# First stage: latents and rotary keys from rounded-32-bit parts, and the next chunk's rows transposed between the rotary queries and the queries' content

## The chip, the core and the metric

The program runs on one core of a Trainium2 chip. The metric is the device time of one launch in microseconds, so lower is better. The engines are TensorE (PE for its matmuls, PEld for its weight loads), VectorE (DVE), ScalarE (ACT), GpSimd (POOL) and SyncE (SP), which issues most DMAs. Each works through its own list of instructions in order, and they meet at semaphores.

## What is computed

An embedding lookup, one attention layer with low-rank (latent) queries, keys and values, and one mixture-of-experts layer, for 4 sequences of 2048 tokens of 256 numbers. All is 32-bit. The part that the change touches is the projection ahead of the attention:

```python
h = take(weight, x)                      # (4, 2048, 256)
n = layernorm(h)
ct_q  = n @ Wd_q + b;    ct_kv = n @ Wd_kv + b            # latents, 128 wide
query = heads(ct_q @ Wu_q + b) + heads(rope(ct_q @ Wq_r + b))
key   = heads(ct_kv @ Wu_k + b) + heads(rope(n @ Wk_r + b))
value = heads(ct_kv @ Wu_v + b_v)
out   = softmax(query key^T / scale) value                # 16 heads of 16
h = h + out @ Wo + b_o
h = h + moe(layernorm(h))                # 32 experts, top 1, 320 slots each
```

## The kernel before

Four stages follow each other: the projections (first stage), the attention, the router, the experts. The time up to about 284 us is the first stage, the attention lasts to about 2914 us, the router to about 3060 us.

**The first stage** goes through 16 chunks of 512 tokens (four sequences b, four chunks k in each; this text numbers them 0 to 15). The orders are written out by hand in one function `chunk` for each engine:

- **POOL**: the two sums of the queries' rotary terms (L395, L396), four gathers of table rows for the chunk three ahead (L357), the low part of the queries (L404, x = 0), the root of the layer norm for the chunk two ahead (`root`: L364, L365, L367, L370), the low part of the keys (L404, x = 1).
- **DVE**: four rotary terms of the queries (L557), the values with their bias (L586), the queries' sum (`full`, L566), the statistics of the chunk two ahead (L545), four rotary terms of the keys (L557), the moments (L549), the two sums of the keys' terms (L598, L599), the keys' sum (L566).
- **ACT**: the copy of the transposed rows (L494), the high part of the queries (`split`, L520), the two latents of the next chunk (L499), the high part of the keys (L520), the normalisation of the chunk two ahead (L507).
- **PE**: rotary queries (L442), the queries' content (L454), values (L459), the transposes of the next chunk's normed rows (L420), rotary keys (L445), the next chunk's latents (L428), the keys' content (L454).
- **SP**: stores the rows, the values (L334) and the parts (L341), each when its semaphore says so.

A query or key leaves the stage as a high part (rounded to fp32r by ACT) and a low part (the rest, by POOL). The low part needs the high part, and the high part needs `full`. The POOL sums of a chunk stand behind the keys' low part of the chunk before. Matmuls on plain 32-bit data show in the trace as two MATMUL records each; those on data marked fp32r (the attention's scores) as one.

**The attention** begins on DVE straight behind its last `full`, with maxima over keys and queries of the first four heads (L1027). POOL multiplies each unit's result by the reciprocals (L824). **The router** has its own `root` on POOL (L1228 to L1234), behind it the scatter of rows to expert slots (L1257).

## Time and profile before

| | us |
|---|---|
| median of 3 runs | 3315.01 |
| lowest and highest | 3313.55 and 3324.78 |
| time of the profiled execution | 3315.87 |
| its span | 3314.0 |

| engine | busy us | share of the span |
|---|---|---|
| PE | 3202.7 | 97% |
| DVE | 2908.6 | 88% |
| ACT | 2468.7 | 74% |
| POOL | 565.3 | 17% |

The profile is one execution. 1.9 us lie around its span. The shares are means over four stages with different limits; the attention alone is four fifths of the time.

### The profile page before, as it was taken

Reading aid. Unit: us, or ns where it says so; the run is one execution under the profiler, and the core shown is the slowest. Engines: PE = TensorE matmul, PEld = TensorE weight load, DVE = VectorE, ACT = ScalarE, POOL = GpSimd, SP = SyncE. Lnnn points to the kernel's source line nnn. Section 1 sums busy time; section 2 is a strip of 40 time slices with the busy share of each in tenths; the row PEclk is TensorE's granted clock in tenths of the full one; section 3 lists DMA queues with packets and bytes.
Section 4 is the critical chain, followed back from the end, with each engine's and each line's share of the span. In section 5 each row is a group of like instructions: output and inputs, shape, how many; then the busy total and the mean of one; then the engine's idle time right before and its main releaser. Section 6 shows DMA issues by size and latency. Waiting matters only on the chain.

```text
span 3314.0 us, 67613 instructions
## 1 busy us (share of the span) xinstructions
PE 3202.7 (97%) x27520; PEld 1369.7 (41%) x27520; DVE 2908.6 (88%) x3157; ACT 2468.7 (74%) x4578; POOL 565.3 (17%) x752
## 2 busy tenths in 40 slices
PE   7997999999999999999999999999999999986999
PEld 3443333333333333333333333333333333365666
DVE  6889999999999999999999999999999999567222
ACT  3331888888888888888888888888888888943221
POOL 7882000000000000000000000000000000046233
PEclk9997999999999999999999999999999999998999
DMA  6895213131313131313131313122222220168773
GB/s 201 256 299 159 54 49 72 37 72 37 72 38 72 38 74 38 72 40 72 37 72 39 83 34 79 39 70 44 65 45 58 45 83 21 37 204 305 231 238 101
DMA packets 269155, 305.40 MB, mean 92 GB/s; under 512 B 45270, under 2 KB 198399, under 8 KB 265517
## 3 DMA queue, kind: packets, MB, share of 16 engines
q1 hardware_dynamic: 256812, 271.63, 29.7%
q0 software_dynamic: 12032, 29.45, 2.7%
q8 instruction: 217, 3.56, 0.5%
q14 instruction: 94, 0.76, 0.1%
HBM read 165.81 MB, written 139.23 MB: 92 GB/s over the span
## 4 chain that ended last, share of the span: by engine, by line
PE 81%; ACT 4%; DVE 3%; issue 2%; POOL 1%; DMA 0%; another core or an unknown queue 0%; SPq 0%; POOLq 0%; DVEq 0%
PE ps_o L916 33%; PE ps_s L899 26%; PE ps_m L868 13%; ACT probs L1012 2%; PE ps_g L1592 2%; PE ps_y L1603 2%; PE ps_u L1592 2%; DVE max_parts L1027 2%; ACT weighted L992 1%; PE ps_td L1581 1%; ACT rows_c L1343 1%; POOL slot_rows L1257 0%; PE ps_s L883 0%; POOL shift_c L1234 0%; DVE stats_c L1377 0%
## 5 line engine op out<-in xcount | busy, mean ns | idle before, releaser
L1027 DVE TENSOR_REDUCE max_parts<-ps_m 128x2 f32<-128x1024 f32 x2048 | 2486.1, 1223 | 79.9 <-PE ps_m L868 71.5
L1012 ACT ACTIVATE probs<-ps_s 128x512 f32<-128x512 f32 x4096 | 2217.5, 597 | 312.3 <-PE ps_s L899 127.8
L868 PE MATMUL ps_m<-keys,queries 48*128 48x512 f32 x4096 | 1483.5, 453 | 17.1 <-DVE max_parts L1027 16.7
L899 PE MATMUL ps_s<-queries,keys 51*128 51x512 f32 x4096 | 1480.5, 447 | 9.5 <-ACT probs L1012 3.1
L916 PE MATMUL ps_o<-probs,vals 128*32 128x256 f32 x16384 | 1295.5, 391 | 0.0
L899 PEld LDWEIGHTS ps_s<-queries,keys 51*128 51x128 f32 x4096 | 610.5, 185 | 832.2 <-issue 785.2
L868 PEld LDWEIGHTS ps_m<-keys,queries 48*128 48x128 f32 x4096 | 595.4, 187 | 77.4 <-DVE max_parts L1027 50.2
L916 PEld LDWEIGHTS ps_o<-probs,vals 128*32 128x32 f32 x16384 | 329.4, 108 | 720.4 <-issue 699.0
L824 POOL TENSOR_TENSOR heads_out<-weighted,recip_rows 128x512 f32<-128x512 f32 x63 | 80.9, 1285 | 2147.4 <-DMA recip_rows<-recip_rows_dram 2147.4
L1663 DVE TENSOR_TENSOR hidden<-ps_u,silu 128x320 f32<-128x320 f32 x64 | 31.5, 492 | 127.4 <-PE ps_u L1592 101.6
L1639 ACT ACTIVATE silu<-ps_g 128x320 f32<-128x320 f32 x64 | 28.0, 438 | 134.1 <-PE ps_g L1592 82.8
L520 ACT ACTIVATE parts<-full 128x1024 fp32r<-128x1024 f32 x32 | 33.8, 1057 | 99.7 <-DVE full L566 79.0
L1565 POOL DMA_INDIRECT out<-result,tokens_d x80 | 77.9, 974 | 172.0 <-DVE result L1669 151.9
L1669 DVE SCALAR_TENSOR_TENSOR result<-ps_y,rows_d 128x256 f32<-128x256 f32 x80 | 38.7, 484 | 53.4 <-PE ps_y L1603 49.6
L404 POOL TENSOR_TENSOR parts<-full,parts 128x1024 fp32r<-128x1024 f32 x32 | 75.6, 2363 | 35.7 <-ACT parts L520 35.3
L1343 ACT ACTIVATE rows_c<-resid,shift_c,rstd_c 128x256 f32<-128x256 f32 x64 | 33.2, 589 | 60.5 <-POOL shift_c L1234 60.5
L1592 PE MATMUL ps_g<-rows_td,w_gate 128*128 128x320 f32 x256 | 77.2, 445 | 0.5 <-issue 0.5
L1603 PE MATMUL ps_y<-w_down,hidden 128*64 128x256 f32 x640 | 75.9, 384 | 0.7 <-DVE hidden L1663 0.7
L1592 PE MATMUL ps_u<-rows_td,w_up 128*128 128x320 f32 x256 | 74.1, 432 | 0.0
L566 DVE SCALAR_TENSOR_TENSOR full<-ps_r,b_cols,sums 128x512 f32<-128x512 f32 x64 | 45.1, 747 | 32.0 <-POOL sums L396 29.4
L1271 PE MATMUL ps_p<-w_o,att_t 128*128 128x256 f32 x256 | 64.2, 396 | 7.1 <-DVE resid L1371 6.9
L1633 ACT ACTIVATE rows_td<-ps_td 128x512 f32<-128x512 f32 (+1 forms) x48 | 23.6, 524 | 61.4 <-PE ps_td L1581 61.4
(108 smaller groups left out, 1600.0 us busy)
## 6 DMA issues: line engine op xcount, KB each, us to landing
slot_rows<-empty SPq DMA_DIRECT2D x16, 1290.0 KB, 5.2
vext<-val SPq DMA_DIRECT2D x64, 256.0 KB
halves_q<-parts SPq DMA_DIRECT2D x64, 256.0 KB
halves_k<-parts SPq DMA_DIRECT2D x64, 256.0 KB
keys<-halves_k SPq DMA_DIRECT2D x32, 512.0 KB, 7.5
queries<-halves_q SPq DMA_DIRECT2D x128, 128.0 KB, 3.2
vals<-vext SPq DMA_DIRECT2D x32, 512.0 KB, 5.6
recip_rows<-recip_rows_dram SPq DMA_DIRECT2D x64, 256.0 KB
```

Source lines behind the costliest of these rows:

```text
L404: pool.tensor_tensor(parts[:, k % 2, x, 1].bitcast(F32R), full[:, x], parts[:, k % 2, x, 0], ALU.subtract).then_inc(low_ok[x], 1)
L824: pool.tensor_tensor(heads_out[:, lu % 2, :], weighted[:, lu % 2, :], recip_rows[:, lu % 2, :], ALU.mult).then_inc(heads_ok, 1)
L868: mm = pe.matmul(ps_m[m % 2][:, h, :], queries_r[par][rows, qt, p, t * P:(t + 1) * P], keys_r[par][rows, p, c * 512:(c + 1) * 512], start= ...
L899: pe.matmul(ps_s[bank][:], keys_r[par][rows, p, k * P:(k + 1) * P], queries_r[par][rows, qt, p, :], start=True, stop=True).then_inc(scores ...
L916: mm = pe.matmul(ps_o[32 * j:32 * j + 32, cols], vals[:, par, k, VW * j:VW * (j + 1)], probs[:, (n + j) % RING, cols], start=k == 0 and ha ...
L1012: act.activation(probs[:, n % RING, :], ps_s[bank][:], ACT.Exp, scale=SCALE).then_inc(probs_ok[bank], 1)
L1027: dve.tensor_reduce(max_parts[:, lu % 2, :, p, t, c], ps_m[m % 2][:], AX.X, ALU.max).then_inc(maxima_ok[m % 2], 1)
L1271: mm = pe.matmul(ps_p[:, t // 2, t % 2 * DM:(t % 2 + 1) * DM], att_t[:, k, d, t * P:(t + 1) * P], w_o[:, d, :], start=d == 0, stop=d == KD ...
L1343: act.activation(rows[:, k, t, 0:DM], resid[:, k % 2, t, :], ACT.Identity, bias=shift[:, k % 2, t:t + 1], scale=rstd[:, k % 2, t:t + 1]).t ...
L1565: pool.indirect_dma_start(out, bass.IndirectOffsetOnAxis(ap=tokens[:, k, i:i + 1], axis=0), result[:, k % 2, i, :], None, bounds_check=T - ...
L1592: mm = pe.matmul(bank[m][:, 0:CAP], w[:, k, KD * e + d, m * P:(m + 1) * P], by_half[:, :, e, :], start=d == 0, stop=d == KD - 1)
L1603: mm = pe.matmul(ps_y[n % 2][e * HALF:(e + 1) * HALF, 0:DM], hidden[:, k % 2, e, f, i * HALF:(i + 1) * HALF], w_down[:, k, (FF // P) * e + ...
```

## The change

1. Latents and rotary keys: weights and transposed rows are split into a rounded part and the rest, both fp32r, and each plain matmul becomes three fp32r ones (high by high, low by high, high by low). ACT writes the high rows in its copy, DVE the low rows in a new step `low_rows`. The weights are split once, by DVE at the start.
2. The values lose their bias in the first stage, and ACT copies them (`copy_val`) in place of DVE. POOL adds the bias to each attention result instead (`add_values_bias`, 64 times), from a small table that SP loads at the start of the attention.
3. The layer norm's two small preparations move from POOL to DVE (`root_inputs`), in the first stage and in the router.
4. POOL in the first stage: `root` goes ahead of both low parts.
5. ACT in the first stage: the keys' high part goes behind the next chunk's copy of transposed rows.
6. PE in the first stage: the next chunk's transposes go between the rotary queries and the queries' content, from chunk 1 on.
7. Router on DVE: the moments go ahead of `gate`, and the new `root_inputs` behind it.

```diff
@@ POOL, first stage
 def root(b, k):
-    pool.wait_ge(stats_ok, after(b, k, CT))
-    pool.tensor_tensor(var_eps[:, k, :], mv[:, k, :, 1], eps_sb[:], ALU.add).then_inc(eps_ok, 1)
-    pool.tensor_tensor(neg_mean[:, k, :], no_mean[:], mv[:, k, :, 0], ALU.subtract).then_inc(neg_mean_ok, 1)
     pool.wait_ge(eps_ok, after(b, k))
     pool.tensor_tensor(rstd[:, k, :], var_eps[:, k, :], neg_half[:], ALU.pow).then_inc(rstd_ok, 1)
...
     if ahead:
         gather(*ahead)
+    if not (last and k + 2 >= CPB):
+        root(*((b, k + 2) if k + 2 < CPB else (b + 1, k + 2 - CPB)))
     for x in range(2):
-        if x == 1 and not (last and k + 2 >= CPB):
-            root(*((b, k + 2) if k + 2 < CPB else (b + 1, k + 2 - CPB)))
         pool.wait_ge(high_ok[x], after(b, k))
@@ PE, latent
     for x in range(2):
         for d in range(KD):
-            last = pe.matmul(ps_l[:, x, :], w_down[:, x, d, :], normed_t[:, k % 2, d, :],
-                             start=d == 0, stop=d == KD - 1)
+            for p in range(2):
+                pe.matmul(ps_l[:, x, :], w_down_r[:, p, x, d, :], high_r[:, k % 2, d, :],
+                          start=d == 0 and p == 0, stop=False, skip_group_check=True)
+    pe.wait_ge(nt_low_ok, after(b, k))
+    for x in range(2):
+        for d in range(KD):
+            last = pe.matmul(ps_l[:, x, :], w_down_r[:, 0, x, d, :], low_r[:, k % 2, d, :],
+                             start=False, stop=d == KD - 1, skip_group_check=True)
         last.then_inc(lat_ps, 1)
@@ PE, chunk
     rotary(b, k, 0)
+    early = more and (b, k) != (0, 0)
+    if early:
+        transpose(*nxt)
     content(b, k, 0)
     values(b, k)
-    if more:
+    if more and not early:
         transpose(*nxt)
@@ ACT, chunk
     if more:
         copy_nt(*nxt)
+    if (b, k) != (0, 0):
+        split(*((b, k - 1) if k else (b - 1, CPB - 1)), 1)
+    copy_val(b, k)
     split(b, k, 0)
     if more:
         copy_lat(*nxt)
-    split(b, k, 1)
@@ DVE, first stage
+def root_inputs(b, k):
+    dve.wait_ge(stats_steps, after(b, k, 2 * CT))
+    dve.tensor_scalar(neg_mean[:, k, :], mv[:, k, :, 0], -1.0, None, ALU.mult)
+    dve.tensor_scalar(var_eps[:, k, :], mv[:, k, :, 1], EPS, None, ALU.add).then_inc(eps_ok, 1)
+def low_rows(b, k):
+    dve.wait_ge(nt_ok, after(b, k))
+    dve.tensor_tensor(low_r[:, k % 2], ps_t[:], normed_h[:, k % 2], ALU.subtract).then_inc(nt_low_ok, 1)
...
+dve.wait_ge(w_in, 3 * 16)
+dve.tensor_copy(w_down_r[:, 0], w_down[:]).then_inc(w_split, 1)
+dve.tensor_copy(w_kr_r[:, 0], w_kr[:]).then_inc(w_split, 1)
...
     rope_terms(b, k, 0)
-    dve.wait_ge(val_out[k % 2], uses(b, k, CT * 16))
-    for h in range(2):
-        ...
+    if not (last and k == CPB - 1):
+        low_rows(*((b, k + 1) if k + 1 < CPB else (b + 1, 0)))
     add_content(b, k, 0)
     if ahead:
         row_stats(*ahead)
+        row_moments(*ahead)
+        root_inputs(*ahead)
     rope_terms(b, k, 1)
-    if ahead:
-        row_moments(*ahead)
@@ POOL, attention
+def add_values_bias(pool, step, lu):
+    q = (step * 2 + lu // 4) % (QUADS // BATCH)
+    pool.tensor_scalar(heads_out[:, lu % 2, :], heads_out[:, lu % 2, :], bias_v[:, q:q + 1], None, ALU.add).then_inc(heads_ok, 1)
```

**POOL, one chunk in the middle of the first stage.** `sums` and `parts` are the sums and low parts, `emb` the gathers. Before:

```order
L395 TENSOR_TENSOR sums<-terms 128x512 [waits terms_ok_q,ids_in0,full_ok_q,emb_out0,norm_ok]
L396 TENSOR_TENSOR sums<-terms 128x512
L357 DMA emb<-in_table,ids 128x256 x4
L404 TENSOR_TENSOR parts<-full,parts 128x1024 [waits high_ok_q]
L364 TENSOR_TENSOR var_eps<-mv,eps_sb 128x4 [waits stats_ok]
L365 TENSOR_TENSOR neg_mean<-no_mean,mv 128x4
L367 TENSOR_TENSOR rstd<-var_eps,neg_half 128x4 [waits eps_ok]
L370 TENSOR_TENSOR shift<-neg_mean,rstd 128x4 [waits neg_mean_ok,rstd_ok]
L404 TENSOR_TENSOR parts<-full,parts 128x1024 [waits high_ok_k]
```

After:

```order
L388 TENSOR_TENSOR sums<-terms 128x512 [waits terms_ok_q,ids_in1,full_ok_q,emb_out1,norm_ok]
L389 TENSOR_TENSOR sums<-terms 128x512
L356 DMA emb<-in_table,ids 128x256 x4
L363 TENSOR_TENSOR rstd<-var_eps,neg_half 128x4 [waits eps_ok]
L365 TENSOR_TENSOR shift<-neg_mean,rstd 128x4 [waits rstd_ok]
L396 TENSOR_TENSOR parts<-full,parts 128x1024 [waits high_ok_q]
L396 TENSOR_TENSOR parts<-full,parts 128x1024 [waits high_ok_k]
```

The root now stands between the gathers and the queries' low part, with two operations fewer.

**ACT, one chunk of the first stage.** `parts` with full_ok_q or full_ok_k is the high part of queries or keys. Before:

```order
L494 ACTIVATE normed_t<-ps_t 128x1024 [waits trans_ok]
L520 ACTIVATE parts<-full 128x1024 [waits parts_out0,full_ok_q]
L499 ACTIVATE lat<-ps_l,b_cols 128x512 [waits lat_ps] x2
L520 ACTIVATE parts<-full 128x1024 [waits parts_out0,full_ok_k]
L507 ACTIVATE normed<-emb,shift,rstd 128x256 [waits trans_ok,shift_ok]
```

After:

```order
L500 ACTIVATE normed_h<-ps_t 128x1024 [waits trans_ok]
L534 ACTIVATE parts<-full 128x1024 [waits parts_out0,full_ok_k]
L506 ACTIVATE val<-ps_l 128x32x16 [waits val_ps,val_out1]
L506 ACTIVATE val<-ps_l 128x32x16 [waits val_ps]
L534 ACTIVATE parts<-full 128x1024 [waits parts_out1,full_ok_q]
L512 ACTIVATE lat<-ps_l,b_cols 128x512 [waits lat_ps] x2
L520 ACTIVATE normed<-emb,shift,rstd 128x256 [waits trans_ok,shift_ok]
```

The keys' high part of a chunk now follows the next chunk's copy of transposed rows.

**PE, from the rotary queries of a chunk on.** Before:

```order
L442 MATMUL ps_r<-lat,w_qr 128x512 [waits lat_ok,terms_ok_k]
L442 MATMUL ps_r<-lat,w_qr 128x512
L454 MATMUL ps_r<-lat,w_uq 128x512 [waits full_ok_k]
L454 MATMUL ps_r<-lat,w_uq 128x512
L459 MATMUL ps_l<-w_uv,lat 128x256 x4
L420 MATMUL ps_t<-ident_a,normed 128x128 [waits nt_ok,norm_ok]
L420 MATMUL ps_t<-ident_a,normed 128x128 x7
L445 MATMUL ps_r<-normed_t,w_kr 128x512 [waits terms_ok_q]
```

After:

```order
L443 MATMUL ps_r<-lat,w_qr 128x512 [waits lat_ok,terms_ok_k]
L443 MATMUL ps_r<-lat,w_qr 128x512
L415 MATMUL ps_t<-ident_a,normed 128x128 [waits nt_low_ok,norm_ok]
L415 MATMUL ps_t<-ident_a,normed 128x128 x7
L456 MATMUL ps_r<-lat,w_uq 128x512 [waits full_ok_k]
L456 MATMUL ps_r<-lat,w_uq 128x512
L461 MATMUL ps_l<-w_uv,lat 128x256 x4
L447 MATMUL ps_r<-normed_h,w_kr_parts 128x512 [waits terms_ok_q]
```

The transposes moved ahead of the content and the values.

## Rows read from the trace of the kernel before

**Rows 1.** Chain of waits in time: start us, length us, engine, line, count.

```profile
284.23 36.21 DVE max_parts L1027 x32
```

**Rows 2.** Timeline, POOL, one period: start us, length us, engine, line, operation [idle before].

```profile
229.84 1.26 POOL L396 TENSOR_TENSOR sums<-terms 128x512 f32<-128x512 f32 x1
...
235.11 0.95 POOL L357 DMA_INDIRECT emb<-in_table,ids  x1 [0.31 <-issue]
236.08 2.35 POOL L404 TENSOR_TENSOR parts<-full,parts 128x1024 fp32r<-128x1024 f32 x1
238.41 0.65 POOL L364 TENSOR_TENSOR var_eps<-mv,eps_sb 128x4 f32<-128x4 f32 x1
...
239.61 1.05 POOL L367 TENSOR_TENSOR rstd<-var_eps,neg_half 128x4 f32<-128x4 f32 x1
240.75 0.20 POOL L370 TENSOR_TENSOR shift<-neg_mean,rstd 128x4 f32<-128x4 f32 x1
242.26 2.37 POOL L404 TENSOR_TENSOR parts<-full,parts 128x1024 fp32r<-128x1024 f32 x1 [1.32 <-ACT parts L520]
...
245.82 1.27 POOL L396 TENSOR_TENSOR sums<-terms 128x512 f32<-128x512 f32 x1
```

**Rows 3.** Timeline, DVE, the same period.

```profile
231.19 1.41 DVE L566 SCALAR_TENSOR_TENSOR full<-ps_r,b_cols,sums 128x512 f32<-128x512 f32 x2 [1.59 <-POOL sums L396]
232.52 1.39 DVE L545 BATCH_NORM_STATS2 stats<-emb 128x6 f32<-128x256 f32 x4
233.95 0.75 DVE L557 SCALAR_TENSOR_TENSOR terms<-ps_r,b_cols,cos_sb 128x512 f32<-128x512 f32 x1
...
236.59 0.37 DVE L549 BATCH_NORM_AGGREGATE mv<-stats 128x2 f32<-128x6 f32 x4
236.88 2.12 DVE L598 TENSOR_TENSOR sums<-terms 128x512 f32<-128x512 f32 x1
...
239.69 1.41 DVE L566 SCALAR_TENSOR_TENSOR full<-ps_r,b_cols,sums 128x512 f32<-128x512 f32 x2
```

**Rows 4.** Timeline, ACT, the end of the same period.

```profile
241.13 1.06 ACT L520 ACTIVATE parts<-full 128x1024 fp32r<-128x1024 f32 x1 [3.79 <-DVE full L566]
242.09 2.06 ACT L507 ACTIVATE normed<-emb,shift,rstd 128x256 f32<-128x256 f32 x4
245.77 1.02 ACT L494 ACTIVATE normed_t<-ps_t 128x1024 f32<-128x1024 f32 x1 [1.62 <-PE ps_t L420]
```

**Rows 5.** Timeline, PE, the end of the same period.

```profile
238.17 1.88 PE L442 MATMUL ps_r<-lat,w_qr 128*128 128x512 f32 x4
241.15 1.99 PE L454 MATMUL ps_r<-lat,w_uq 128*128 128x512 f32 x4 [1.10 <-DVE full L566]
...
244.70 1.04 PE L420 MATMUL ps_t<-ident_a,normed 128*128 128x128 f32 x8
```

**Rows 6.** One line's instructions: durations ns (lowest/median/highest), first and last start.

```profile
L598 DVE TENSOR_TENSOR sums<-terms x16: 658/2118/2135, 41.5 to 280.6; 128x512 f32<-128x512 f32 x16
```

**Rows 7.** The same view, the attention's score matmuls on fp32r data.

```profile
L899 PE MATMUL ps_s<-queries,keys x4096: 386/492/792, 326.3 to 2910.8; 51*128 51x512 f32 x196
```

**Rows 8.** Timeline, POOL, the second sum of chunks 7 and 8.

```profile
146.30 1.27 POOL L396 TENSOR_TENSOR sums<-terms 128x512 f32<-128x512 f32 x1
...
165.86 1.26 POOL L396 TENSOR_TENSOR sums<-terms 128x512 f32<-128x512 f32 x1
```

**Rows 9.** Timeline, PE, the one late rotary of the queries.

```profile
172.75 3.50 PE L442 MATMUL ps_r<-lat,w_qr 128*128 128x512 f32 x4 [1.96 <-issue]
```

**Rows 10.** Stretch: length, busy us (count) of PE, PEld, DVE, ACT, POOL; granted clock, DMA share, GB/s.

```profile
174.00:176.00 2.00, 2.00 (x3) 0.34 (x1) 1.91 (x3) 0.00 (x0) 2.00 (x4) 0.50 0.94 272
```

**Rows 11.** Timeline, router, all engines: the DVE base sum and the POOL shift beside it.

```profile
2968.88 1.22 DVE L1386 TENSOR_TENSOR rows_c<-resid,rows_c 128x1024 f32<-128x1024 f32 x1
...
2969.30 0.85 POOL L1234 TENSOR_TENSOR shift_c<-neg_mean_c,rstd_c 128x4 f32<-128x4 f32 x1
```

**Rows 12.** Timeline, PE, the latents of chunk 0.

```profile
20.65 6.47 PE L428 MATMUL ps_l<-normed_t,w_down_qkv 128*128 128x512 f32 x8 [1.21 <-ACT normed_t L494]
```

More of the change, by code:

```diff
@@ L756, in _ @@
             first_heads.load_ones(sp, keys[1])
+            sp.wait_ge(bias_set, 1)
+            for j in range(QUAD):
+                src = dram["b_v"].rearrange("a (q j d) -> j d (a q)", j=QUAD, d=HD)[j]
+                sp.dma_start(bias_v[VW * j:VW * j + HD, :], src, allow_slow_non_contiguous=True).then_inc(bias_in, 16)
             max_rows(0, 0)
@@ L1466, in chunk @@
                     row_stats(*n)
-                    dve.wait_ge(stats_raw, after(*n, CT))
+                    dve.wait_ge(stats_steps, after(*n, 2 * CT) - CT)
+                if more:
+                    row_moments(*n)
                 gate(b, k)
                 if more:
-                    row_moments(*n)
+                    root_inputs(*n)
                 counts(b, k)
```

147 lines of the change are left out of this document (78 added, 69 removed).

## The prediction

> **What bounds the kernel now.** I read first where the first stage hands over. In the chain of waits in time [rows 1] the attention opens with 32 maxima on DVE back to back, from 284.23 us, straight behind DVE's last `full` of the first stage. So whatever the first stage gives or takes on DVE moves the rest one for one. Then I read one period of that stage, engine by engine. From the end of one second sum on POOL (229.84 + 1.26 = 231.10) to the end of the next (245.82 + 1.27 = 247.09) it is 15.99 us [rows 2]. PE is not what sets this: in each period it stands 1.10 us before the queries' content, waiting for DVE [rows 5]. Following each waiting step to its releaser gives a closed loop: POOL sums, DVE `full` (231.19), statistics (232.52), key terms (233.95 to 236.59), moments, two key sums, `full` (239.69) [rows 3], ACT high part (241.13) [rows 4], POOL low part (242.26), POOL sums [rows 2]. Within it sits one stall. The first key sum takes 2.12 us, its lowest is 0.658 us [rows 3, 6], and it ends as the queries' low part ends on POOL (236.08 + 2.35 = 238.43) [rows 2]. Both read two tensors from SBUF, and the one that began first holds the other off. Matmul time is outside the loop.
>
> **The change, part by part.** I count from the end of a second POOL sum as 0.
>
> *PE's work.* A plain 128x512 matmul is two records. Four records take 1.88 us [rows 5]; with a tail of 0.17 us on the last one, a record is 0.43 us. The latents and the rotary keys have eight records each, 3.44 us. An fp32r matmul of 512 columns has a lowest record of 0.386 us, tail included [rows 7], so it costs 0.22 us at least and 0.39 us at most. Twelve of them take 2.6 to 4.7 us. I take 2.6, since the lowest record is one with nothing beside it: 1.7 us less a chunk in all. At the high end it is 2.5 us more a chunk, of which PE's slack of 1.1 us hides a part. As PE waits for the loop, the gain is worth nothing there; what it leaves is a longer idle PE.
>
> *DVE's work.* Out goes the values' bias add, in comes `low_rows`, 1024 columns with one operand in PSUM: about 1.1 us (between the 1.22 us of a 128x1024 sum in the router [rows 11] and its own share of 0.66 us per 512 columns in `full` [rows 3]). Both lie between the query terms and `full`, where DVE waits 1.59 us for POOL [rows 3], so this is hidden. The moments only change place within the loop. `root_inputs` is new in it: two 128x4 operations and two waits, 0.1 to 0.7 us by the nearest rows (a quarter of the four moments' 0.37 us, and the 0.65 us of the same operation on POOL [rows 2, 3]); I take 0.3. The key sums then come at 0.09 + 1.33 + 1.43 + 0.3 (moments) + 0.3 + 2.64 = 6.1 us.
>
> *POOL's order.* The last gather ends at 4.96 us. The root is now next: 1.14 us from `rstd` to `shift`, 0.20 for `shift` [rows 2]. So the queries' low part is ready to start at 6.3 us instead of 4.98, 0.2 us behind the arrival of the key sums. Before, it had a lead of 0.8 us on them (236.08 against 236.88) [rows 2, 3] and cost them 1.46 us. Now the two meet. If the first key sum gets in, the low part comes between the two key sums and the second waits for all of it; if not, the first waits. Either way about 2.3 us are lost where 1.46 were: the low part ends near 9.0 to 9.2, and `full` starts 1.28 us behind it if both sums still follow (as 238.41 to 239.69), less if one does: at about 10.0.
>
> The Trainium skill, page "SBUF — State Buffer", section "Who interferes with whom", says that the shared port pair is an exclusive lock, taken by whichever of the two starts first, for the whole instruction, and that a VectorE operation with two SBUF inputs is held off by a GpSimd operation that reads SBUF. The 2.12 us row agrees with it. By it alone a lead of 0.2 us would give both key sums free passage only if the lock were kept between them; the sum would then be that of the second case below.
>
> *The rest of the loop.* `full` 1.44 us to ACT's start, 11.4; high part to POOL's start 1.13, 12.6; low part 2.32, 14.9; two sums 2.51, **17.4 us** [rows 2 to 4]. A second loop is new. The keys' high part on ACT now stands behind the copy of the next chunk's rows, which need the transposes, the normalisation and the root: shift ends 6.3, normalisation 2.1 (8.4), transposes with tail 1.07 (9.5), copy 1.02 (10.6), high part 1.15 (11.7), low part 2.32, sums 2.51: **16.6 us** [rows 2, 4, 5]. This one cannot be passed. So the period is 16.6 at least; I take 17.3 (the first loop, less a tenth for waits counted twice). Had the transposes stayed behind the values, they would wait for PE's content, which waits for `full`, and the loop would be some 5 us longer; that is what the move is needed for, not a gain.
>
> *How many periods.* Thirteen intervals between second sums have gathers in them (chunks 0 to 13). Twelve are 16.0 us, one 19.56 [rows 8], where POOL waits for the rows' store behind the queued loads of the first keys. +1.3 times 13 is +16.9 us. The one long interval has its DMA overdue by 3.56 us; a longer period hides 1.3 of it: -1.3. The last two intervals have no gathers: the first gets about +1.3 by the second loop, the last about -0.8, since there is nothing left to transpose: +0.5.
>
> *The start.* The first latents take eight records at the lower clock in 6.47 us [rows 12]; twelve fp32r ones at half rate take 12 x 0.43 = 5.2, with `low_rows` done beside the first eight: -1.0. The weight splits on DVE run before the first rows have landed.
>
> The Trainium skill, page "SBUF — State Buffer", section "SBUF: two separate sides", warns that an fp32 tensor_copy within SBUF on VectorE keeps GpSimd from writing its gather descriptors. The two weight copies would do that. An estimate from "VectorE: DVE Perf Modes", (58 + 256) cycles at 0.96 GHz each, is 0.7 us; with it the forecast would be 0.7 us higher. No run here shows it.
>
> *Values' bias in the attention.* 64 more POOL operations of 128x512, 1.3 us each by the nearest row, the sum with two tensors [rows 2]. POOL is idle for 83% of the span and the result is stored long before its next use, so 0. If nothing covered them it would be 64 x 1.3 = 83 us; I see no waiter for that.
>
> *The router.* POOL loses two small operations, DVE gains two. There the base sum on DVE (from 2968.88) holds POOL's shift for 0.65 us [rows 11], once in two chunks. `rstd` can start about 0.2 us sooner and the base comes 0.3 later, so the shift may just get ahead: 8 pairs of chunks by -0.8 to +0.3 us, -6 to +2. I take -2.
>
> **Sum**, against the profiled execution (3315.87 us, 0.9 above the median of the runs shown): +16.9 - 1.3 + 0.5 - 1.0 + 0 - 2 = +13, and from the median 3315.0 that is **3328 us**.
>
> **The rivals.**
> - *Only the second loop binds* (A2): the key sums pass POOL's low part together. 13 x 0.6 = 7.8, less 1.3, plus 0.5, less 1, less 2: +4, **3319 us**. For it: the key sums arrive 0.2 us ahead. Against: each key sum is an instruction of its own and POOL stands ready between them.
> - *PE's clock* (C), slower than before by more than can be mistaken. After PE stood idle for 1.96 us its next four records took 3.50 us in place of 1.88, and the granted clock of that stretch was 0.50, the 1.2 GHz level [rows 9, 10]. In the changed kernel PE idles in every chunk: about 0.5 us before the transposes, 2 before the content, 1.7 before the rotary queries. A slow stretch of 4 us costs nothing, as the rotary keys have 3 us of slack; it decides from about 8 us on, content, values and rotary keys all at half speed: then the transposes of the next chunk come some 3.5 us late, the high part 1.4, and the period is 18.7. 13 x 2.7 = 35, less 3.8: **3346 us**. Against: dense work stands between the gaps, and the clock is at the upper level in all other chunks.
> - *PE bound after all* (D): if the waits I followed are loose and the period is PE's work plus its wait, it falls from 16.0 by 1.7 to 14.3: 13 x -1.7 = -22, less 3: **3290 us**. Against: no step of the loop is shortened by the change.
> - *The change doesn't do what it says*: the parts could cost as much as plain matmuls (0.39 us each). Then PE fills its slack, and the time is that of the forecast or of the clock's case.
>
> **How the numbers follow.** Forecast 0.50, A2 0.17, C 0.17, D 0.09, and 0.07 for what I don't see, on both sides. A measurement of this kernel tells a difference of about 0.5% (16.6 us) from none. Faster than 3298.4: D and 0.02, 0.11. Slower than 3331.6: C, 0.12 of the forecast (unknowns of the router, of `root_inputs` and of the port all high), and 0.02, 0.31. The rest, 0.58, is within. The range from 3314 (A2 with the router's whole gain) to 3348 (C's middle) leaves out D, half of C and the remainder, under 0.2.
>
> **What would show it.** Right: the second POOL sums 17.3 us apart, one of the two key sums at 2.5 to 3 us, DVE's maxima beginning near 299 us, PE with some 4 us idle a chunk at the upper clock. The second loop: ACT's high part of the keys starts as its copy ends. C: granted clock near 0.75 in the first stage and records of 0.8 us. Wrong altogether: sums less than 16 us apart, or the gain or loss in the attention, whose units keep their length by this account.

## The result and the profile after

The changed kernel takes 3335.0 us (median, 3331.6 to 3361.4) beside 3313.6 us for the kernel before: ratio 1.0081, 95% interval 1.005 to 1.0113. The forecast was 3328, 13 us over the 3315.0 measured until then; against the 3313.6 us here the change costs 21.4.

| stretch, us | before, profiled | after, profiled | difference |
|---|---|---|---|
| start to DVE's first maximum | 284.2 | 299.1 | +14.9 |
| first maximum to the first weighted sum | 92.4 | 118.7 | +26.3 |
| first weighted sum to the last | 2537.0 | 2543.2 | +6.2 |
| last weighted sum to the experts' first transposes | 154.9 | 151.5 | -3.4 |
| the rest | 245.5 | 245.6 | +0.1 |
| span | 3314.0 | 3358.1 | +44.1 |

The profiled execution of the changed kernel is one of its two longest (3360.0 us), and the second line of the table is why. A shorter one stands in the experiments below (e1_again). I take the first stage first. The chain of waits in time begins the attention here, as [rows 1] did before:

```profile
299.10 36.21 DVE max_parts L1069 x32
```

One period on POOL, timeline (start us, length us, engine, line, operation, idle before it), to be read against [rows 2]:

```profile
225.97 1.30 POOL L389 TENSOR_TENSOR sums<-terms 128x512 f32<-128x512 f32 x1
...
232.22 1.05 POOL L363 TENSOR_TENSOR rstd<-var_eps,neg_half 128x4 f32<-128x4 f32 x1
233.36 0.19 POOL L365 TENSOR_TENSOR shift<-neg_mean,rstd 128x4 f32<-128x4 f32 x1
233.51 2.84 POOL L396 TENSOR_TENSOR parts<-full,parts 128x1024 fp32r<-128x1024 f32 x1
239.57 2.37 POOL L396 TENSOR_TENSOR parts<-full,parts 128x1024 fp32r<-128x1024 f32 x1 [3.22 <-ACT parts L534]
...
243.13 1.31 POOL L389 TENSOR_TENSOR sums<-terms 128x512 f32<-128x512 f32 x1
```

From end to end of a second sum it is 17.17 us (227.27 to 244.44), where it was 15.99. DVE and ACT in the same period, timelines, against [rows 3] and [rows 4]:

```profile
233.43 0.69 DVE L625 TENSOR_TENSOR sums<-terms 128x512 f32<-128x512 f32 x1
234.04 2.86 DVE L626 TENSOR_TENSOR sums<-terms 128x512 f32<-128x512 f32 x1
236.99 1.41 DVE L588 SCALAR_TENSOR_TENSOR full<-ps_r,b_cols,sums 128x512 f32<-128x512 f32 x2
```

```profile
236.85 1.02 ACT L500 ACTIVATE normed_h<-ps_t 128x1024 fp32r<-128x1024 f32 x1 [1.18 <-PE ps_t L415]
238.43 1.06 ACT L534 ACTIVATE parts<-full 128x1024 fp32r<-128x1024 f32 x1 [0.56 <-DVE full L588]
```

The first key sum and the queries' low part overlap by 0.6 us at their start (233.43 and 233.51), and the low part takes 2.84 us for its usual 2.36. Then the low part goes on and the second key sum takes 2.86 us, until just after the low part ends (236.35). ACT's high part of the keys starts when `full` is there, 0.56 us after the copy ended: the loop through the key sums binds, and the second loop, through root and transposes, is 0.56 us shorter.

The other part of the profile is the opening of the attention. Stretches of all engines, before and then after (length, busy us with counts of PE, PEld, DVE, ACT and POOL, granted clock, DMA share, GB/s):

```profile
330.00:340.00 10.00, 10.00 (x69) 4.67 (x69) 8.36 (x8) 6.86 (x13) 0.00 (x0) 0.65 0.01 2
340.00:350.00 10.00, 9.93 (x94) 3.67 (x96) 9.98 (x9) 8.12 (x16) 0.00 (x0) 1.00 0.00 0
```

```profile
299.00:340.00 41.00, 28.03 (x71) 10.17 (x71) 40.97 (x39) 1.33 (x2) 3.27 (x6) 0.50 0.27 80
350.00:360.00 10.00, 10.00 (x58) 3.64 (x54) 6.03 (x5) 4.34 (x8) 0.00 (x0) 0.50 0.01 2
400.00:410.00 10.00, 10.00 (x58) 3.30 (x52) 5.59 (x5) 4.62 (x10) 0.00 (x0) 0.50 1.02 159
420.00:430.00 10.00, 10.00 (x96) 3.68 (x96) 8.60 (x8) 7.28 (x15) 0.00 (x0) 0.90 0.01 2
```

In both kernels the granted clock falls to 0.50 (1.2 GHz) at the hand-over. PE has by then made its first four matmuls of the maxima and stands idle until DVE begins to take them, 4.79 us in the kernel before and 4.80 us here. PE's timeline, before and after:

```profile
285.42 0.57 PE L868 MATMUL ps_m<-keys,queries 48*128 48x512 f32 x2 [4.79 <-DVE max_parts L1027]
```

```profile
300.29 0.79 PE L910 MATMUL ps_m<-keys,queries 48*128 48x512 f32 x2 [4.80 <-DVE max_parts L1069]
```

Behind it DVE's maxima set the pace and PE is busy 28 of 41 us. In the kernel before the clock is back at 1.00 (2.4 GHz) at 336.9 us, 10.6 us after the last gap of PE (the 0.65 for 330 to 340 us is a mean over both levels). In this execution of the changed kernel PE has no gap from 341.3 us on and stays at 0.50 until 422 us, with 58 matmuls per 10 us instead of 94 to 96. That is the 26 us.

### The profile page after: what moved, and what is told of

It reads as the page before. It is cut to its first block, busy times and chain, and to the rows that moved or that the text cites. A ratio compares the mean times of both kernels' runs of the same rounds, so it can differ in the third digit from the quotient of the medians.

```text
span 3358.1 us, 67896 instructions
## 1 busy us (share of the span) xinstructions
PE 3228.7 (96%) x27648; PEld 1407.6 (42%) x27648; DVE 2926.9 (87%) x3209; ACT 2487.1 (74%) x4610; POOL 648.7 (19%) x749
## 4 chain that ended last, share of the span: by engine, by line
PE 81%; ACT 4%; DVE 3%; issue 1%; DMA 1%; POOL 0%; SPq 0%; POOLq 0%; DVEq 0%
PE ps_o L958 34%; PE ps_s L941 27%; PE ps_m L910 12%; ACT probs L1054 2%; PE ps_g L1633 2%; PE ps_y L1644 2%; PE ps_u L1633 2%; ACT weighted L1034 1%; DVE max_parts L1069 1%; DMA att_t<-att 1%; PE ps_td L1622 1%; DVE stats_c L1410 0%; DVE resid L1404 0%; PE ps_s L925 0%; PE ps_p L1304 0%
## 5 line engine op out<-in xcount | busy, mean ns | idle before, releaser
L910 PE MATMUL ps_m<-keys,queries 48*128 48x512 f32 x4096 | 1504.5, 458 | 16.6 <-DVE max_parts L1069 16.5
L941 PE MATMUL ps_s<-queries,keys 51*128 51x512 f32 x4096 | 1499.0, 452 | 9.7 <-ACT probs L1054 3.1
L958 PE MATMUL ps_o<-probs,vals 128*32 128x256 f32 x16384 | 1309.5, 395 | 0.0
L910 PEld LDWEIGHTS ps_m<-keys,queries 48*128 48x128 f32 x4096 | 602.8, 189 | 77.3 <-DVE max_parts L1069 47.1
L838 POOL TENSOR_SCALAR heads_out<-heads_out,bias_v 128x512 f32<-128x512 f32 x64 | 100.2, 1566 | 6.3
```

Source lines behind the costliest of these rows:

```text
L838: pool.tensor_scalar(heads_out[:, lu % 2, :], heads_out[:, lu % 2, :], bias_v[:, q:q + 1], None, ALU.add).then_inc(heads_ok, 1)
L910: mm = pe.matmul(ps_m[m % 2][:, h, :], queries_r[par][rows, qt, p, t * P:(t + 1) * P], keys_r[par][rows, p, c * 512:(c + 1) * 512], start= ...
L941: pe.matmul(ps_s[bank][:], keys_r[par][rows, p, k * P:(k + 1) * P], queries_r[par][rows, qt, p, :], start=True, stop=True).then_inc(scores ...
L958: mm = pe.matmul(ps_o[32 * j:32 * j + 32, cols], vals[:, par, k, VW * j:VW * (j + 1)], probs[:, (n + j) % RING, cols], start=k == 0 and ha ...
```

## The experiments

Where a kernel's numbers are compared, I use three: the distance of second sums on POOL (the period), DVE's first maximum (the hand-over), and the time from the first weighted sum to the last. The ratio is always to the kernel before on the same chip.

**The changed kernel again.** No edit.

> The changed kernel as it is, once more, to see what its shorter times look like in the trace: its profiled run took 3360.0 us at a mean granted clock of 0.973, most of its others 3332 to 3336 at 0.982 to 0.985. Theory 1 (the clock holds the spread): the first stage hands over near 299 us again and the sums stand 17.15 us apart; whatever is over or under 3333 lies in the attention's opening, in the length of the stretch at a granted clock of 0.50 (about 120 us of it in the 3360 us run, about 50 us in the kernel before), at roughly 0.37 us for each us of it. Theory 2 (the attention itself is longer, by the added bias operation on POOL): every unit of the attention is longer by about 0.1 to 0.5 us also where the granted clock is 1.00.

Median 3340.3 us (3334.4 to 3347.1), ratio 1.0071 (1.005 to 1.0093). Period 17.15, hand-over 298.4. In its profiled execution (3343.3 us) the upper clock returns at 376 us, 35.5 us after PE's last gap. Stretches, then ACT's weighted sums (durations ns lowest/median/highest, first and last start):

```profile
360.00:370.00 10.00, 10.00 (x60) 3.50 (x54) 6.97 (x6) 4.76 (x9) 0.00 (x0) 0.50 0.00 0
370.00:380.00 10.00, 10.00 (x70) 3.60 (x74) 7.03 (x7) 5.67 (x11) 0.00 (x0) 0.70 0.01 2
```

```profile
L1034 ACT ACTIVATE weighted<-ps_o x64: 597/605/606, 400.6 to 2941.0; 128x512 f32<-128x512 f32 x64
```

From hand-over to first weighted sum it is 102.2 us, beside 118.7 above and 92.4 in the kernel before. The clock's return at 336.9, 376 and 422 us is 53, 78 and 123 us behind the hand-over: 16.5 us for 45, 10 for 25, so some 0.37 us lost for each us at the lower clock. From the first weighted sum to the last it is 2540.4 us, 3.4 more than before at a clock of 1.00 throughout. Theory 1 holds for the spread. The attention is also longer where the clock is at 1.00, as theory 2 has it; whether the bias operation is the cause is asked further down.

**The key sums ahead of the low parts.**

```diff
     for x in range(2):
         pool.wait_ge(high_ok[x], after(b, k))
+        if x == 0:
+            pool.wait_ge(sums_ok[1], after(b, k, 2))
```

> The changed kernel with one wait more: POOL begins the queries' low parts only when DVE has written both key sums. Theory (the second key sum's 2.9 us are time spent behind POOL's low parts, and they lie in the loop that binds): the second key sum falls from 2.86 to about 0.65 us, the low parts start some 1.3 us later, which costs nothing as the keys' low parts wait 3.2 us for ACT anyway, and the loop that binds loses about 2.2 us. The second loop (root, normalise, transposes, copy, keys' high parts), which had 0.56 us to spare per 17.15 us, then takes over: period 16.5 to 16.7 us, 0.5 to 0.65 us less over 13 periods, 7 to 9 us off the hand-over (290 to 292 us), total about 8 us under the changed kernel. Rival (the key sum's time is its own, or another engine binds right behind): period stays at 17.1 or more, key sum at 2.9 us. Rival (the second loop isn't near): period falls to about 15 us, 28 us off.

The key sums now take 0.69 and 0.68 us, so the 2.2 us were time behind the low part. The hand-over only comes to 296.3 us, though, and misses the 290 to 292 of the theory, since periods of 16.5 and 17.7 us take turns: median 3335.9 us, ratio 1.0055 (1.0035 to 1.0074). POOL's and PE's timelines and one stretch show what tells the two apart:

```profile
223.84 1.28 POOL L389 TENSOR_TENSOR sums<-terms 128x512 f32<-128x512 f32 x1
240.33 1.30 POOL L389 TENSOR_TENSOR sums<-terms 128x512 f32<-128x512 f32 x1
258.04 1.30 POOL L389 TENSOR_TENSOR sums<-terms 128x512 f32<-128x512 f32 x1
```

```profile
231.29 1.98 PE L445 MATMUL ps_r<-lat,w_qr 128*128 128x512 f32 x4 [2.37 <-DVE terms L581]
...
247.81 3.68 PE L445 MATMUL ps_r<-lat,w_qr 128*128 128x512 f32 x4 [2.36 <-DVE terms L581]
```

```profile
248.00:250.00 2.00, 2.00 (x3) 0.96 (x4) 1.91 (x4) 2.00 (x4) 0.77 (x1) 0.50 1.11 370
```

The short period (to 240.33) has its rotary queries at the upper clock, in the long one (to 258.04) they take 3.68 us at 0.50, and the transposes behind them come 1.2 us late. The second loop binds now, and it has PE in it. PE stands idle in front of both, for 2.37 and 2.36 us (1.12 in the changed kernel, whose clock stays up), so the length of the gap alone does not say in which of these periods the clock falls. This is the forecast's case of PE's clock, in a small form: it costs 1.2 us in one period of two as soon as there is no slack behind the rotary queries.

**The same with PE's gap filled.** The wait of the run above stays, and eight matmuls are added, into the transposes' bank:

```diff
+    if (b, k) != (0, 0):
+        for i in range(8):
+            pe.matmul(ps_t[:, i % 2, :], w_kr_r[:, 0, 0, 0:P], high_r[:, k % 2, 0, :], start=True, stop=True)
     rotary(b, k, 0)
```

> The kernel with the key sums ahead of the low parts (period 16.5 and 17.7 us in turn, hand-over 296.3 us), with eight matmuls more in PE's idle 2.4 us ahead of the rotary queries, into the transposes' bank. Theory (the 17.7 us periods are those in which the granted clock falls to 0.50 for 3.4 us while PE makes the rotary queries and the transposes on the second loop, and it falls because PE is idle before them): the granted clock stays at 1.00, all periods are 16.5 us, the hand-over comes near 289 to 291 us, total 6 us under that kernel. Rival (the periods of 17.7 us come from something else, such as the order in which transfers land): they stay, and the eight matmuls either cost nothing or, where the clock is 0.50, delay the rotary queries by up to 1.5 us.

Theory met: 16.5 us in every ordinary period but the first (17.36) and the one behind the long one (16.62), hand-over 290.7, which is 5.6 us earlier. The median is 3329.5 us, ratio 1.0038 (1.0025 to 1.0052) beside 1.0055; the two intervals overlap, and it is the traces that tell the kernels apart. PE's timeline and the stretch:

```profile
240.41 2.43 PE L479 MATMUL ps_t<-normed_h,w_kr_parts 128*128 128x512 f32 x8
243.34 1.98 PE L445 MATMUL ps_r<-lat,w_qr 128*128 128x512 f32 x4 [0.50 <-DVE terms L584]
```

```profile
190.00:265.00 75.00, 71.31 (x271) 46.73 (x270) 58.44 (x120) 35.24 (x53) 51.32 (x43) 1.00 0.87 263
```

Over the same 75 us the kernel without the filling has a mean granted clock of 0.93. Useless work on PE brought the hand-over forward, since it keeps the clock at 1.00. And 16.52 us is the second loop, measured.

**The root back between the low parts.**

```diff
-    if not (last and k + 2 >= CPB):
-        root(*((b, k + 2) if k + 2 < CPB else (b + 1, k + 2 - CPB)))
     for x in range(2):
+        if x == 1 and not (last and k + 2 >= CPB):
+            root(*((b, k + 2) if k + 2 < CPB else (b + 1, k + 2 - CPB)))
         pool.wait_ge(high_ok[x], after(b, k))
```

> The changed kernel with the root put back between the queries' and the keys' low parts on POOL, nothing else. Theory (a second loop root, normalise, transposes, copy, keys' high parts, keys' low parts, sums now exists, since the keys' high parts stand behind the copy of the next chunk's transposed rows): the root starts about 2.8 us later in the period, the second loop, at 16.6 us, becomes the one that binds, near 19.5 to 20 us; hand-over 34 to 38 us later than the changed kernel's 299 us. Rival (no such loop: the root's place only changes which operations meet on DVE and POOL): period within 0.3 us of 17.15 us, as the low parts of the queries would meet the key sums about as before.

Theory met: period 19.3 to 20.2 us, hand-over 334.1 (+35), median 3368.7, ratio 1.0155 (1.0138 to 1.0172). POOL's timeline shows the keys' low part waiting 6.22 us for ACT (3.22 in the changed kernel):

```profile
240.35 1.52 POOL L363 TENSOR_TENSOR rstd<-var_eps,neg_half 128x4 f32<-128x4 f32 x1
241.96 0.19 POOL L365 TENSOR_TENSOR shift<-neg_mean,rstd 128x4 f32<-128x4 f32 x1
248.37 2.36 POOL L397 TENSOR_TENSOR parts<-full,parts 128x1024 fp32r<-128x1024 f32 x1 [6.22 <-ACT parts L535]
```

**The keys' high part back in its own chunk.**

```diff
-    if (b, k) != (0, 0):
-        split(*((b, k - 1) if k else (b - 1, CPB - 1)), 1)
     copy_val(b, k)
     split(b, k, 0)
     if more:
         copy_lat(*nxt)
+    split(b, k, 1)
...
-split(BATCH - 1, CPB - 1, 1)
```

> The changed kernel with ACT's high parts of the keys back in their own chunk, behind the latents' copies, nothing else. Theory (the second loop goes with it; the first loop stays, ACT's high parts start when DVE has the keys' full, or when the latents' copies are done): period 17.2 to 17.6 us, hand-over 0 to 6 us later than the changed kernel's. Rival (moving the high parts ahead of the next chunk's work is what pays for the early transposes): period over 18 us.

Theory missed, the rival holds: periods from 17.1 to 19.4 us, 18.2 in the mean, hand-over 317.7 (+19), median 3351.1 us, ratio 1.0099 (1.0079 to 1.012). I had left PE out. ACT normalises the next rows only behind the keys' high part, and PE, which is in order, stands with the early transposes in front of the queries' content. ACT's and PE's timelines:

```profile
228.90 1.06 ACT L534 ACTIVATE parts<-full 128x1024 fp32r<-128x1024 f32 x1 [2.37 <-DVE full L586]
229.87 2.06 ACT L520 ACTIVATE normed<-emb,shift,rstd 128x256 f32<-128x256 f32 x4
```

```profile
231.98 1.72 PE L415 MATMUL ps_t<-ident_a,normed 128*128 128x128 f32 x8 [2.85 <-ACT normed L520]
233.50 2.98 PE L456 MATMUL ps_r<-lat,w_uq 128*128 128x512 f32 x4
```

The 2.98 us for four records that take 1.88 are the lower clock again (a mean of 0.57 from 232 to 236 us).

**The arithmetic alone, all three moves undone** (root between the low parts, keys' high part in its own chunk, and):

```diff
-    early = more and (b, k) != (0, 0)
+    early = False
```

> The changed kernel's arithmetic in the order of the kernel before: latents and rotary keys from rounded parts, the row copy's rounding error made by DVE, values copied by ACT, but the transposes behind the values again, ACT's high parts of the keys in their own chunk, the root between POOL's two low parts. Theory (no loop through the transposes is left; the one through the key sums, the high and the low parts is longer than the kernel before's 16.0 us by the two instructions for the root's inputs and a key sum that is still caught by the low parts): period 16.9 to 17.3 us, hand-over within 3 us of the changed kernel's 298 us, so that the three moves of order together bring nothing. Rival (the moves of order pay for a part of what the parts cost): period 18 us or more, hand-over 10 us or more behind the changed kernel's. Rival (the parts cost nothing and all of the loss lies in the order): 16.0 us, 284 us.

The last rival is nearly what came: period 16.00 us, hand-over 286.1, median 3321.7 us, ratio 1.002 (1.0003 to 1.0037). In the old order the rest of the change, the arithmetic with the root's inputs and the moments on DVE, thus costs 2 us in the first stage, and the three moves together cost the other 12 to 13. The 2 us are not in the period: the last two intervals take 32.3 us together (29.3 in the kernel before), the start is 1.4 us shorter. The two runs above each undid one move and made things worse (+35 and +19 us); undoing all three made them 13 us better. The moves lean on each other, and one at a time they cannot be judged. My 16.9 to 17.3 had a key sum of 2.9 us in it; here the low part begins 1.97 us ahead of the first key sum and is nearly done. DVE's timeline:

```profile
237.07 0.95 DVE L624 TENSOR_TENSOR sums<-terms 128x512 f32<-128x512 f32 x1
237.95 0.68 DVE L625 TENSOR_TENSOR sums<-terms 128x512 f32<-128x512 f32 x1
```

**The same arithmetic, late transposes, root ahead and key sums first** (POOL's wait of e2_sums_first, `early = False`, the high part in its own chunk).

> The changed kernel with the transposes behind the values again, the keys' high parts in their own chunk (so that neither loop through the transposes is left), the root where the change put it, and POOL's low parts held until both key sums are written. Theory (the key sums' 2.2 us behind the low parts were on the only loop left): key sums 0.68 us each, period 15.5 to 16.0 us, hand-over 276 to 282 us, 3 to 8 us ahead of the kernel before; total 3310 to 3318 us. Rival (PE, with the transposes waiting for the normalised rows in the middle of the chunk, or the clock that falls while it waits, takes over): 16.5 us or more.

Period 15.74 us, in the range of the theory, but by another loop. The hand-over at 282.3 and the median of 3318.7 us lie just above its ranges, with one long interval of 21.44 us; ratio 1.0005 (0.9992 to 1.0018), the time of the kernel before. DVE's timeline:

```profile
228.79 1.22 DVE L593 TENSOR_TENSOR normed_l<-ps_t,normed_h 128x1024 fp32r<-128x1024 f32 x1 [3.10 <-ACT normed_h L502]
229.94 1.40 DVE L588 SCALAR_TENSOR_TENSOR full<-ps_r,b_cols,sums 128x512 f32<-128x512 f32 x2
```

`full` no longer waits for POOL's sums (ended 229.09) but for `low_rows` in front of it, which waits for ACT's copy of the transposed rows, which wait for PE's values and content, which wait for the last `full`. The kernel with the parts alone has the same loop with 0.26 us more of key sum: 16.00 - 0.26 = 15.74. `low_rows` is therefore not hidden once the transposes stay late; in the changed kernel, with early transposes, it stands ahead of DVE's wait (240.95 to 242.16, `full` from 244.53) and the second loop is the price.

**The attention without the added bias.** The values' bias is in neither place here, so this part of the computation is missing. The division is cut to one operation in both places where it stands; one is shown:

```diff
-pool.tensor_tensor(heads_out[:, lu % 2, :], weighted[:, lu % 2, :], recip_rows[:, lu % 2, :], ALU.mult).then_inc(divided, 1)
-pool.wait_ge(divided, step * UNITS + lu + 1)
-add_values_bias(pool, step, lu)
+pool.tensor_tensor(heads_out[:, lu % 2, :], weighted[:, lu % 2, :], recip_rows[:, lu % 2, :], ALU.mult).then_inc(heads_ok, 1)
```

> The changed kernel with the values' bias left out of the attention altogether (the bias is in neither place, so that part of the computation is missing): POOL's added operation after each unit's division, 64 times 1.57 us, is gone. Theory 1 (the added operation costs nothing, the attention is longer only where the granted clock stays at 0.50 in its opening): from the first weighted sum to the last it takes 2540 to 2543 us, as in the changed kernel, and the time stays within 0.2% of it (3333 to 3345 us). Theory 2 (the added operation is what makes the units longer): that stretch returns to the 2537 us of the kernel before, 3 to 6 us off; and if it also has a part in the opening's long stretch at the lower clock, that falls from 79 to 123 us to the 51 us of the kernel before, 10 to 25 us off.

First weighted sum to last 2540.7 us, median 3334.4, ratio 1.0054 (1.0034 to 1.0074): theory 1. POOL's 64 additions of 1.57 us cost nothing that can be measured. The opening takes 92.2 us here, as in the kernel before.

**The attention's code of the kernel before** on the changed first stage (the values' bias is missing here too, with its table and the loads of it).

```diff
-neg_steps = sem("neg_steps")
+neg_1 = sem("neg_1")
+neg_r1 = sem("neg_r1")
+neg_2 = sem("neg_2")
...
-pool.memset(bias_v[:], 0.0).then_inc(bias_set, 1)
-pool.wait_ge(bias_in, QUAD * 16)
...
-add_values_bias(pool, step, lu)
```

> The changed kernel with the whole attention code of the kernel before: its semaphores for the maxima's split as before, no bias loaded and none added (the first stage doesn't add it either, so the values' bias is missing). In seven kernels with the change's first stage and attention, the stretch from the first weighted sum to the last took 2540.0 to 2543.2 us, without the added bias operation too; in three with the code of the kernel before 2535.8 to 2538.8 us. Theory 1 (the 4 us come from the attention's code, such as the one semaphore that POOL's four steps now share): 2535 to 2539 us here. Theory 2 (they come from what the first stage leaves behind: where its buffers and rows lie, and the moment at which it ends): 2540 to 2543 us. Either way the first stage keeps its period of 17.15 us and hands over at 297 to 299 us.

```profile
L1018 ACT ACTIVATE weighted<-ps_o x64: 598/604/604, 393.7 to 2932.0; 128x512 f32<-128x512 f32 x64
```

2538.3 us, median 3329.3, ratio 1.0038 (1.0024 to 1.0052): in the range of theory 1. The hand-over, at 301.1 us, is later than expected, behind a long interval of 22.5 us. Four profiles with the attention's code of before have 2535.8 to 2538.8 us from first weighted sum to last, ten with the changed code 2540.0 to 2543.2, 3.8 us apart in the mean. The groups do not overlap, but each spreads by 3 us and the step between them is 1.2, and only this one profile has the old code behind the changed first stage. That the attention's code costs some 4 us is therefore likely, not shown. As the bias operation is not the cause, the shared semaphore or the bias table's loads would be left; these two were not told apart.

**Two matmuls more behind each pair of the opening.** They need finished keys, so two waits of PE move ahead of the opening.

```diff
+pe.wait_ge(stage.terms_ok[1], 4 * NCH)
+pe.wait_ge(stage.full_ok[1], 2 * NCH)
 for n in range(-LEAD, TURN_LEAD - LEAD):
     maximum(0, n, 1)
     maximum(0, n, 0)
+    for i in range(2):
+        pe.matmul(ps_s[0][:], keys_r[0][0:SROWS, 0, 0:P], queries_r[0][0:SROWS, 0, 0, :], start=True, stop=True)
```

> The changed kernel with two matmuls more behind each of the 35 pairs of the attention's opening, in which PE otherwise is 70% busy at a granted clock of 0.50 and DVE's maxima (1.0 us each) are the bound; their output goes to a bank that is not in use yet. Theory 1 (the lower clock in the opening is an answer to PE's idle time there, and lasts on into the full stretch behind it by 30 to 80 us of the changed kernel's): with PE busy nearly throughout, the granted clock stays at 1.00 or comes back during the opening, the attention's beginning up to its first weighted sum falls from 102 to 119 us to about 90 to 95 us, and the time to 3325 to 3332 us with less spread. Theory 2 (the lower clock is an answer to the busy time, or comes whatever PE does): it stays at 0.50, four matmuls then take about 1.7 us per maximum instead of 1.0, and the opening is some 20 to 25 us longer: 3355 us or more.

Neither theory: median 3340.2 us (3338.4 to 3370.4), ratio 1.0087 (1.0059 to 1.0116), 98.2 us to the first weighted sum. Stretches:

```profile
300.00:340.00 40.00, 40.00 (x127) 33.83 (x126) 38.28 (x33) 0.00 (x0) 1.44 (x2) 0.50 0.21 63
340.00:350.00 10.00, 8.41 (x28) 5.42 (x29) 8.85 (x9) 2.42 (x6) 0.87 (x4) 0.50 0.23 61
350.00:360.00 10.00, 10.00 (x61) 4.70 (x59) 8.36 (x8) 6.52 (x13) 0.00 (x0) 0.62 0.01 3
```

The moved waits left PE idle for 4.38 us (293.7 to 298.1, until DVE's last `full`), and the clock fell in that gap, ahead of the first added matmul. So the run does not show what filling the idle time of the hand-over itself would do. What it shows is that PE, busy from 298.1 to 344.7 us without a gap, did not get the clock back in 46 us; it came at 357.7 us, 10.6 us after the next gaps, as in the kernel before. What brings the clock back there is not PE's busy time by itself, as the profile counts it. The Trainium skill, page "TensorE: Matmul & The Clock Gate", section "What's actually happening", has the lower level as the default and activity as what releases it. The filled gap of the first stage agrees; this stretch does not, and the measurement decides.

**The kernel before, with the key sums ahead of the low parts.** The edit of e2_sums_first on the kernel before.

> The kernel before with one wait more: POOL begins the queries' low parts only when DVE has written both key sums. In the kernel before the first key sum takes 2.12 us behind those low parts, in the loop that binds (period 16.00 us). Theory: both key sums take 0.68 us, 1.44 us off that loop; POOL's low parts start about 0.9 us later and the root behind them too, so the keys' low parts, which now find the root ended only 0.2 us after ACT's high parts, take back a part: period 14.8 to 15.7 us, 5 to 15 us off the hand-over (284 us), total 3300 to 3309 us. Rival (the later low parts and root delay the keys' low parts by all that was gained): period 16.0 us, no change.

The rival holds: key sums 0.66 and 0.69 us, but a period of 15.90 (16.00 before) and the hand-over at 284.7. POOL's wait, low part, root and keys' low part in one row take back what the sums gave. The median is 3324.3 us, ratio 1.0025 (1.0004 to 1.0045), with executions from 3315.2 us at a mean granted clock of 0.986 to 3341.4 at 0.976: a lower mean clock with a longer time is thus no property of the changed kernel alone.

**The kernel before, root ahead of both low parts as well**, and on DVE the moments ahead of the key terms, as in the changed kernel.

```diff
@@ POOL
+    if not (last and k + 2 >= CPB):
+        root(*((b, k + 2) if k + 2 < CPB else (b + 1, k + 2 - CPB)))
     for x in range(2):
-        if x == 1 and not (last and k + 2 >= CPB):
-            root(*((b, k + 2) if k + 2 < CPB else (b + 1, k + 2 - CPB)))
         pool.wait_ge(high_ok[x], after(b, k))
+        if x == 0:
+            pool.wait_ge(sums_ok[1], after(b, k, 2))
@@ DVE
+    row_moments(*ahead)
     rope_terms(b, k, 1)
-    row_moments(*ahead)
```

> The kernel before, with nothing of the change's arithmetic: POOL takes the root ahead of the queries' low parts, DVE the moments ahead of the key terms, and the low parts wait until both key sums are written. It takes both ends of what the kernel before with that wait alone showed: there the low parts, the root (1.6 us) and the keys' low parts stood in one row behind the wait and gave 15.9 us. Theory: the root now fills the wait, the keys' low parts start when ACT's high parts are there; the loop is 14.6 us, shorter than PE's own work of 14.9 us and its 1 us of waiting for normalised rows, which shrinks as the root comes earlier: period 15.0 to 15.3 us, 9 to 13 us off the hand-over (271 to 275 us), total 3300 to 3306 us, ahead of both kernels. Rival (PE's wait for the normalised rows stays at 1 us, or the lower clock comes with PE's shorter periods): 15.9 us, no change.

Period 14.67 us, hand-over 270.1 (-14.1), both a little better than expected, median 3304.4 us (3302.6 to 3304.7), ratio 0.9956 (0.9943 to 0.997): ahead of both kernels. POOL's timeline and a stretch:

```profile
224.52 0.22 POOL L370 TENSOR_TENSOR shift<-neg_mean,rstd 128x4 f32<-128x4 f32 x1
225.44 2.37 POOL L405 TENSOR_TENSOR parts<-full,parts 128x1024 fp32r<-128x1024 f32 x1 [0.69 <-DVE sums L599]
227.96 2.37 POOL L405 TENSOR_TENSOR parts<-full,parts 128x1024 fp32r<-128x1024 f32 x1 [0.16 <-ACT parts L521]
```

```profile
182.00:245.00 63.00, 63.00 (x191) 32.89 (x190) 54.00 (x103) 28.94 (x41) 50.78 (x47) 1.00 0.97 297
```

The root fills the wait, the keys' low part starts 0.16 us after ACT, PE has no gap left, and the clock is at 1.00. The kernel before lost time to the order on POOL and DVE, not to its matmuls. The root's move and that of the moments were not tried apart.

This run and the one with late transposes, root ahead and key sums first have the same order and differ by the rest of the change: 14.67 us a period with plain matmuls, 15.74 with the parts, 270.1 against 282.3 us at the hand-over, ratio 0.9956 (0.9943 to 0.997) against 1.0005 (0.9992 to 1.0018) on one chip. So the parts cost 2 us in the old order and 12 in the better one, where `full` waits for `low_rows`.

## Why the prediction was right, and where it was not

The forecast's case is what happened in the first stage, by its mechanism, and 3335.0 us lies in the range. The change cost 21.4 us where +13 was forecast. Of the 8 us between, some 4 lie in the attention, priced at 0, and 2 in the router, where no gain can be seen; the rest is not told apart.

- **First loop 17.4, taken 17.3.** Measured 17.15. The key sums came 6.16 us into the period for 6.1, the low part was ready at 6.24 for 6.3, `full` began at 9.7 for 10.0. The step that carried it, the key sums and the low part meeting with one of the sums held for 2.5 to 3 us, shows as 2.86 us. The key sums got in first by 0.08 us, and the lock was not kept between the two. The Trainium skill's rule (page "SBUF — State Buffer", section "Who interferes with whom", one holder for a whole instruction) is borne out on both sides: 2.84 us for the low part held at its start, 2.86 us for the sum held by it, 0.68 us when they do not meet.
- **Second loop 16.6.** Its terms add up to 16.5. Measured 16.52 once the first was out of the way and the clock was held. But "only the second loop binds" was priced at a steady 16.6; without a filled gap it came out at 16.5 and 17.7 in turn.
- **PE's work, 1.7 us less a chunk.** The twelve latent matmuls on parts take 2.81 us (227.64 to 230.45), not 2.6, where eight records of plain ones take 3.44. With PE idle for 3.0 us of 17.15 (1.12, 0.28 and 1.64) where some 4 were foreseen, its work is 14.1 us a chunk beside 14.9 before, 0.8 less. It moved nothing, as PE's work was outside the loop that binds.
- **Thirteen intervals: +16.9, -1.3, +0.5, start -1.0.** Measured, from the starts of the second sums: twelve ordinary ones +14.2, the long one +1.5 (21.05 against 19.56), the last two +0.4, the start -1.2, in all +14.9 for +15.1. That the sum agrees so well is luck: twelve intervals at +1.3 would be +15.6 and came 1.4 us lower, and the long interval, put at nothing, came 1.5 us higher. The long interval is the term that failed: I had it absorb the longer period. In five profiles with a period of 17.15 us it is 19.6 to 22.5 us, so its overdue transfer is not of a fixed size.
- **"That is what the move is needed for, not a gain".** Wrong. With all three moves undone the period is 16.00 us. The 5 us loop that I feared for late transposes needs the keys' high part already moved behind the copy; late transposes with that move in place were not run, so this loop is argued only. I had costed the transposes' move against the other two moves and never the three together against none; that question was worth 12 us.
- **Values' bias in the attention, 0.** Right, by the kernel without it. "The units keep their length" was off by 3.8 us over 64 units, from something else, most likely in the attention's code.
- **Router -2.** The profiles of the changed router give 151.5 to 158.1 us, those of the old one 154.1 to 154.9. Nothing can be said of 2 us.
- **PE's clock** was weighed in the first stage, where it cost little in this kernel, and not at the attention's opening, where it moves an execution by up to 26 us. That part is not steady: mean granted clocks of 0.984 go with 3333, 0.978 with 3350, 0.973 with 3360 us. What decides how long the lower clock lasts there is open. PE's busy time by itself does not; the one profile without the bias operation had a short opening (92.2 us), but so had five with it, so nothing follows for that operation. Long executions are rarer in the kernel before: of the 21 beside the last runs two took over 3325 us, but five of the ten with the key sums first did; what lengthened those was not profiled.

Of the 21 us at the median, 14 to 15 are the first stage and some 4 the attention. The 2 to 3 that are left are no more than what the clock and the router do from one execution to the next.

## What to carry to other kernels

When a change makes one operation cheaper and moves three others to suit it, cost the cheap operation alone first: here it lost 2 us in the old order, and the moves 12 more. Undo such moves together as well as one by one, since the two that were undone singly each looked needed. And price the operation again in the best order found: there the parts cost 12 us. Where two engines hold each other off, look for something useful for one of them to do while the other finishes (the root, here): a wait alone moved the loss to the next step (15.90 us), the wait and the moves of root and moments together took 14 us off. Before an edit takes slack from in front of PE, look at how long PE then stands idle.

## What was not expected of the hardware

- Eight superfluous matmuls of 2.43 us in all, in a gap of PE, brought the end of the first stage 5.6 us forward by holding the granted clock at 1.00; the next four records took 1.98 us, and 3.68 at 0.50.
- PE busy for 40.00 of 40 us at a granted clock of 0.50, and in another execution busy without a gap from 341.3 to 422 us before the clock came back, where 10.6 us were enough in the kernel before. In both the clock had fallen in a gap of 4.4 to 4.8 us.
- A us at the lower clock in the attention costs 0.37 us, not 0.5. PE is not alone in setting the pace at the upper level, where DVE too is busy for 9.3 to 10 of 10 us (6 of 10 at the lower).
